# A graph kernel whose scalar engine forms part of the one-hot matrices

## The reference

```python
h = relu(layernorm(x)); x = x + L0(h)   # cosine similarity of both ends times edge weights, coeff[...] mix
h = relu(layernorm(x)); x = x + L1(h)   # three rounds of degree-normalised sums (LightGCN)
h = relu(layernorm(x)); x = x + L2(h)   # relu(x[src]) summed, two dense layers
h = relu(layernorm(x)); x = x + L3(h)   # sigmoid(edge_feature @ W_edge) gated mean
```

## Time and profile before

| | |
|---|---|
| median of 3 runs | 1308.59 us (1307.52 to 1309.86) |
| the profiled execution, its own time | 1321.73 us |
| its span, first to last instruction | 1319.8 us |
| mean granted clock of TensorE | 0.895 of full |
| busy: PE, DVE, ACT, POOL | 1060.3, 961.5, 632.8, 169.9 us |

### The profile page before, as it was taken

How to read it: one execution, slowest core, us unless ns; L and a number is a source line. 1 busy time by engine, 2 the same in 40 slices (tenths; PEclk the granted TensorE clock), 3 DMA queues, 4 the chain that set the end, 5 groups by cost and what they waited for, 6 DMA issues and landing times. The chain is left out here.

```text
span 1319.8 us, 36746 instructions
## 1 busy us (share of the span) xinstructions
PE 1060.3 (80%) x15699; PEld 797.3 (60%) x15699; DVE 961.5 (73%) x1434; ACT 632.8 (48%) x2058; POOL 169.9 (13%) x315
## 2 busy tenths in 40 slices
PE   1971558888887888888887888569999897999997
PEld 0620346666665666666665666369999885644553
DVE  8872389999999999999999998566669524233333
ACT  1830445555555555555555555189993212222222
POOL 4604411211112111211121111000000000000000
PEclk9795569988989998899998899679999897799999
DMA  9822301231123111221122111394000150266641
GB/s 227 220 38 32 98 28 77 101 128 77 77 81 147 78 77 77 119 110 77 77 108 120 77 77 77 120 396 188 2 2 2 74 227 2 80 227 242 249 150 25
DMA packets 37355, 144.82 MB, mean 110 GB/s; under 512 B 21148, under 2 KB 21692, under 8 KB 30268
## 3 DMA queue, kind: packets, MB, share of 16 engines
q1 hardware_dynamic: 32012, 133.20, 27.5%
q0 software_dynamic: 2912, 7.92, 2.2%
q10 hardware_dynamic: 2256, 1.23, 0.4%
HBM read 78.63 MB, written 63.71 MB: 108 GB/s over the span
## 5 line engine op out<-in xcount | busy, mean ns | idle before, releaser
L888 ACT ACTIVATE b_c_row<-b_ps 128x300 bf16<-128x300 f32 (+1 forms) x275 | 114.8, 417 | 244.9 <-PE b_ps L1073 229.3
L1286 PE MATMUL layers_ps<-layers_u,layers_c 128*128 128x192 bf16 x2500 | 213.6, 249 | 9.2 <-ACT layers_u L1465 6.7
L1073 PE MATMUL b_ps<-b_mv,b_soh 64*128 64x50 bf16 (+1 forms) x9600 | 202.8, 193 | 21.8 <-issue 12.0
L1073 PEld LDWEIGHTS b_ps<-b_mv,b_soh 64*128 64x128 bf16 x9600 | 172.7, 97 | 77.0 <-issue 43.3
L1286 PEld LDWEIGHTS layers_ps<-layers_u,layers_c 128*128 128x128 bf16 x2500 | 210.1, 99 | 15.0 <-DVE layers_y L1594 8.0
L1126 PE MATMUL b_ps<-k_ident,b_a_row 128*128 128x128 f32 x625 | 116.7, 309 | 89.6 <-DVE b_scale L999 88.5
L1073 PE MATMUL b_ps<-b_u_b,b_y 128*128 128x64 f32 x1250 | 164.8, 283 | 12.5 <-DVE b_y L1013 12.5
L1126 PEld LDWEIGHTS b_ps<-k_ident,b_a_row 128*128 128x128 f32 x625 | 73.6, 152 | 154.6 <-DVE b_scale L999 128.4
L1073 PEld LDWEIGHTS b_ps<-b_u_b,b_y 128*128 128x128 f32 x1250 | 151.1, 196 | 18.8 <-DVE b_y L1013 15.7
L976 DVE TENSOR_TENSOR b_mv<-b_mv,b_parts 128x2808 bf16<-128x2808 bf16 x100 | 149.3, 1493 | 0.0
L1741 DVE COPY layers_c<-layers_ps 128x512 f32<-128x512 f32 (+1 forms) x87 | 55.4, 637 | 117.8 <-PE layers_ps L1420 117.8
(11 more groups left out here) (253 smaller groups left out, 1146.9 us busy)
## 6 DMA issues: line engine op xcount, KB each, us to landing
g_blocks<-b_g_row SPq DMA_DIRECT2D x25, 1600.0 KB, 7.6
layers_c<-g_blocks SPq DMA_DIRECT2D x25, 1600.0 KB, 6.9
c_blocks<-b_c_row SPq DMA_DIRECT2D x25, 800.0 KB, 3.4
layers_c<-c_blocks SPq DMA_DIRECT2D x12, 1600.0 KB, 26.3
prep_attr<-in_edge_attr SPq DMA_DIRECT2D x2, 1883.0 KB
prep_attr<-in_edge_attr SPq DMA_DIRECT2D x1, 1876.0 KB
rec<-sort_rec SPq DMA_DIRECT2D x1, 1209.0 KB
layers_c<-c_blocks SPq DMA_DIRECT2D x1, 800.0 KB, 25.5
```

The source lines that it names most:

```text
L888: nc.scalar.activation(out, src[:, :, at, :, :], ACT.Copy).then_inc(s["evac"], 1)
L1073: return nc.tensor.matmul(out, lhsT, rhs, start=start, stop=True, skip_group_check=True)
L1286: return nc.tensor.matmul(out_, lhsT, rhs, start=start, stop=True, skip_group_check=True)
```

## The change

The low one-hots of the last quarter (10 columns) are no longer compared by DVE. POOL writes the negated low parts of those 10 columns to a small float tile `minus`. ACT then forms, for each of the columns, the square of (number minus low part), ten instructions of 128 elements, in place in `soh[1]`, and one instruction over all 1280 elements takes one minus that and rectifies it: 1 where the number is the low part, 0 elsewhere. In a step the squares are put behind the evacuation of lot 5 (five) and behind `positive` 2 (five), the last instruction behind the evacuation of lot 6. In block 0 all eleven stand behind the evacuation of lot 5. PE waits for the result ahead of lot 9. Elsewhere three semaphores are merged into others, with the same order of work.

```diff
+        minus = l.sb("minus", [P, OH[3][1] - OH[3][0]])
...
                 pool.wait_ge(s["onehot"], 4 * w + (o + 1))
+                if o == 3:
+                    if not (isinstance(w, int) and w == 0):
+                        pool.wait_ge(s["whole"], w)
+                    nc.gpsimd.tensor_tensor(minus[:, :], zero[:, 0:1].to_broadcast([P, n]),
+                                            cols(fld, b, lo, n)[:, 1, :], ALU.subtract).then_inc(s["lows"], 1)
...
+            def distances(w, c0, c1):
+                if c0 == 0:
+                    act.wait_ge(s["lows"], w + 1)
+                    act.wait_ge(s["lot"], NL * w + (ENDS[1] + NL))
+                for c in range(c0, c1):
+                    nc.scalar.activation(soh[1][:, c, :], k["numbers"][:, 0:P], ACT.Square, bias=minus[:, c:c + 1]).then_inc(s["near"], 1)
+
+            def equal(w):
+                n = OH[3][1] - OH[3][0]
+                act.wait_ge(s["near"], n * w + n)
+                nc.scalar.activation(soh[1][:, 0:n, :], soh[1][:, 0:n, :], ACT.Relu, bias=k["ones"][:, 0:1], scale=-1.0
+                                     ).then_inc(s["whole"], 1)
...
                     evacuate(r, w, 0, i)
+                    if i == 5:
+                        distances(w, 0, 10)
+                        equal(w)
...
                         evacuate(r, w, par, i)
+                        if i == 5:
+                            distances(w, 0, 5)
+                        if i == 6:
+                            equal(w)
                     if what == "sims":
                         positive(w - 1, i)
+                        if i == 2:
+                            distances(w, 5, 10)
...
-                nc.vector.tensor_tensor(halves(soh[b][:, 0:n, :]), nums(P), twice(1, P), ALU.is_equal)
+                if o < 3:
+                    nc.vector.tensor_tensor(halves(soh[b][:, 0:n, :]), nums(P), twice(1, P), ALU.is_equal)
...
                     pe.wait_ge(s["onehot"], 4 * w + (o + 3))
+                    if o == 3:
+                        pe.wait_ge(s["whole"], w + 1)
```

More of the change, by code:

```diff
@@ L192, in prepare @@
         names = ("iota const zero dst src weight attr param x dense cparam kept order find edge norm coefs gdiag whd rdiag "
-                 "compared signed tail stored firsts shift turned hd_act wht_pe whd_pe gate row_pe exp ln exps stds nrs "
-                 "sigmoid wht_act row_act scaled attr1 attr2")
+                 "compared signed tail stored shift turned hd_act wht_pe whd_pe gate exp ln exps stds nrs "
+                 "sigmoid wht_act scaled attr1 attr2")
         s = {n: l.sem(n) for n in names.split()}
@@ L323, in _ @@
             for i, (a, n) in enumerate(cuts):
-                act.wait_ge(s["row_pe"], i + 1)
-                nc.scalar.activation(rn_row[:, a:a + n], ps[:, 6 + i % 2, 0:n], ACT.Copy).then_inc(s["row_act"], 1)
+                act.wait_ge(s["wht_pe"], len(cuts) + i + 1)
+                nc.scalar.activation(rn_row[:, a:a + n], ps[:, 6 + i % 2, 0:n], ACT.Copy).then_inc(s["wht_act"], 1)
         @block.tensor
@@ L330, in _ @@
             pe.wait_ge(s["find"], 2)
-            nc.tensor.matmul(ps[:, 0, 0:P], k["ones"][:], diag[:], start=True, stop=True).then_inc(s["firsts"], 1)
+            nc.tensor.matmul(ps[:, 0, 0:P], k["ones"][:], diag[:], start=True, stop=True).then_inc(s["shift"], 1)
             pe.wait_ge(s["order"], 3)
@@ L369, in _ @@
                 if i >= 2:
-                    pe.wait_ge(s["row_act"], i - 1)
-                nc.tensor.matmul(ps[:, 6 + i % 2, 0:n], k["ones"][:], rdiag[:, i, 0:n], start=True, stop=True).then_inc(s["row_pe"], 1)
+                    pe.wait_ge(s["wht_act"], len(cuts) + i - 1)
+                nc.tensor.matmul(ps[:, 6 + i % 2, 0:n], k["ones"][:], rdiag[:, i, 0:n], start=True, stop=True).then_inc(s["wht_pe"], 1)
         @block.vector
@@ L405, in _ @@
             o(v.memset(z[:, T - 1:T], 0.0))
-            dve.wait_ge(s["firsts"], 1)
+            dve.wait_ge(s["shift"], 1)
             shape = [P, 2 * NJ, P]
@@ L411, in _ @@
             f(v.tensor_copy(at[:], line[:]))
-            dve.wait_ge(s["shift"], 1)
+            dve.wait_ge(s["shift"], 2)
             o(v.tensor_tensor(z[0:P - 1, T - 1:T], df[0:P - 1, T - 1:T], ps[0:P - 1, 1, 0:1], ALU.is_gt))
             o(v.tensor_reduce(total[:, 0:1], z[:], AX.X, ALU.add))
-            dve.wait_ge(s["shift"], 2)
+            dve.wait_ge(s["shift"], 3)
             o(v.tensor_scalar(total[:, 1:2], ps[:, 1, 0:1], 1.0, None, ALU.min))
@@ L523, in _ @@
             w(v.scalar_tensor_tensor(uD[:, :, :], whD[:, :, :], coef[:, 3:4], rn[:, :, None].to_broadcast(full), ALU.mult, ALU.mult))
-            dve.wait_ge(s["row_act"], len(cuts))
+            dve.wait_ge(s["wht_act"], 2 * len(cuts))
 def node_of(nc, c, rec, node):
@@ L687, in build @@
         names = ("index turned split rounded doubled hot onehot lot evac sims pos sgn weights made at scaled propped added "
-                 "gate deg degs peak rounds")
+                 "gate deg degs peak rounds lows near whole")
         s = {n: l.sem(n) for n in names.split()}
```

## The result

The changed kernel takes 1312.56 us (median of 20 runs), the kernel before, beside it, 1309.39 (20 runs). The ratio is 1.0023, with a 95% interval of 1.0013 to 1.0034: 3.0 us slower, between 1.7 and 4.5. The prediction said 1312.6 us and slower by over 0.2%.

What follows compares the result with a forecast made beforehand. In the steps it took PE's chain, not DVE (94% busy), to decide when `add` 1 starts. Steps 0, block 0 +4.0 and clock 0 on the median of 1308.59 gave 1312.6 us, range 1309.5 to 1317.

Steps and rivals of the forecast that it cites:

- DVE's instruction: Steps: removing DVE's comparison gains 0, at most 17.5 us; the wait ahead of `add` 1 grows from 0.75 to 1.48 us.
- The prices on ACT: ACT's new work: square pitch 0.28 us, bounds 0.20 and 0.38; rectifier 1.36 us, pitch 1.26; some 4.1 us a block.
- Room in the steps: Steps: ACT's new work costs 0, bounds 0 and 12 us; evacuation of lot 7 ends 0.9 us before lot 9.
- Block 0: Block 0: nothing hides ACT's eleven instructions between the evacuations of lots 5 and 6; +4.0 us, bounds 3.0 and 4.6.
- follows from there in one chain: End of block 0: after `turn_in` 2, at +4.3 us, DVE's split and the first step follow in one chain.
- The rival of a hidden delay: Block 0: faster ACT, transposes at high clock and a good clock pattern hide the delay; 1310.0 us, chance 0.20.
- The clock in the steps: Steps: a later start can change which steps the low clock stretches fall in; 0, bounds -0.8 to +1.0 us.
- DVE as the bound: Steps, at `add` 1: DVE is the bound, 0.73 us a step gained; 1295.1 us, chance 0.07 in whole or part.
- ACT awaited: Steps: ACT becomes the one awaited, 0.1 to 0.5 us a step, 2.4 to 12 us; 1315 to 1325, chance 0.13.
- The table load: Block 0: if the loaded table serves no square, one load of 1.28 us is added; 1313.9 us, chance 0.07.

Runs made afterwards that it cites:

- Two runs with more squares: Changed kernel with three, then eight more squares a step on ACT, into columns not read: 1320.58 us (ratio 1.0103) and 1361.09 us (1.0387).
- second profile: The kernel before, unchanged, profiled again: span 1307.0 us, with no PE wait for issue in block 0.
- `scale` 4 moved: DVE's `scale` 4 put ahead of `add` 1: kernel before 1298.77 us (0.9854), changed kernel 1304.34 us (0.9891); kernel before on another chip 1295.74 us (0.9893).
- steps-only: Changed kernel with block 0's comparison given back to DVE, the 24 steps keeping the new work: 1309.02 us, ratio 1.0010.
- block-0-only: Changed kernel with squares and rectifier taken out of the steps, DVE comparing there, block 0 keeping the new work: 1310.44 us, ratio 1.0025.
- comparison-less: Kernel before with DVE's comparison of the last quarter left out in the 24 steps, nothing in its place: 1308.90 us, ratio 1.0014.
- two entries moved: DVE's `scale` 4 and `sim` 2 both put ahead of `add` 1: kernel before 1323.78 us (1.0038), changed kernel 1325.28 us (1.0048).

## Why the prediction was right, point by point

**DVE's instruction: 0.** Right, and shown by itself. The stretch from `similar` 1 to `add` 1 kept its 5.66 us and the wait went from 0.75 to 1.48, the number that the prediction gave. Leaving the comparison out altogether gave 1.0014 (1.0000 to 1.0027). The busy share of 94% would have misled, the wait did not.

**The prices on ACT.** A square was priced at 0.38 us and is busy for 0.425; its pitch, which is what counts, was 0.28 and is 0.29. The rectifier was 1.36 and is 1.36 to 1.42. Together 4.1 predicted; in block 0, with the wait between them, 4.2 predicted and 4.32 measured. The formula of the Trainium skill, "ScalarE: Activation LUTs", section "What ACT_TABLE_LOAD costs", would have given a pitch of 0.29 and 1.35 for the rectifier, and the trace agrees; for the busy time of a square it gives 0.39, too low like the estimate. No table load came.

**Room in the steps.** Predicted 0.9 us ahead of lot 9; in the trace after, the evacuation of lot 7 ends at 512.94 + 0.48 = 513.42 and lot 9 starts at 514.24, 0.8. Lot 9 is 9.17 us behind `similar` 1, as it was before. Two runs with more squares bear out that the room ends there, though with three of them the price came through the clock, which the prediction's bound for this rival held without naming it.

**Block 0: +4.0.** The mechanism was right, shown by the two halves of the change and the traces; the term was mis-sized. `turn_in` 2 came 9.24 us behind the evacuation of lot 5, 4.2 more than the 5.01 of the first profile (evacuation of lot 5 at 154.30), but 3.7 more than the 5.55 of the second. The transposes gave back 1.1, where I took 0.3 off a delay of 4.3. So DVE's split was 2.6 us later against the second profile, 3.3 against the first. The lower bound of 3.0 was too high for executions without waits for issue ahead of this block. For those with them it was fair: on the second chip, where the profiles have them, it is 31.36 us from the evacuation of lot 5 to the first `similar` 0 in the kernel before with `scale` 4 moved, and 35.52 in the changed one with it, 4.2 more.

One link was wrong as well: that the first step "follows from there in one chain". The next `turn_in` also waits for its DMA, so of the delay at the split 1.3 us (against the steps-only kernel) to 2.6 us (against the second profile) reached the steps. The rival of a hidden delay didn't name this, and it came true in part.

**The clock in the steps: 0, bounds -0.8 to +1.0.** The bounds were too narrow for a single execution. The 23 steps from the first `similar` 0 to the 24th take 616.2 and 616.3 us in the two profiles of the kernel before, 618.2 in the one after, and 617.0, 619.7 and 619.1 in the steps-only, the block-0-only and the comparison-less kernel. `similar` 1 to `similar` 3 is 10.47 or 10.48 us in nearly all of them (10.56 and 10.73 once each in the changed kernel). It isn't that the clock was lower: its mean over these steps is 0.94 in the three longest and 0.93 in the three shortest. What differs is where its low stretches fall. Two stretches of the changed kernel, in the columns of the earlier trace rows:

```profile
200.50:207.30 6.80, 5.97 (x84) 3.75 (x85) 6.45 (x8) 2.17 (x4) 0.59 (x3) 0.50 0.36 144
255.10:282.40 27.30, 21.59 (x505) 16.84 (x499) 25.72 (x33) 19.46 (x51) 5.13 (x14) 1.00 0.28 116
```

The first begins 0.7 us ahead of a `similar` 0, and the time from there to the next `similar` 0 is 28.1 us; the second holds a whole step of 26.0. In the six profiles a low stretch of 3.4 us that begins up to 1.9 us behind `similar` 0 goes with 27.0 or 27.1 us, one of 6.8 us around it with 28.0 to 28.2, one of 6.8 us at the end of a step with 26.4 or 26.5, and one of 3.4 us that begins 5 us ahead of `similar` 0 with 26.0 (26.3 once), like none at all. A different start of the steps deals them out differently.

So some 1.9 us of the changed kernel's time can be this, beside 1.3 to 2.6 of block 0. How these 1.9 us stand in the median of many executions wasn't seen, as each kernel was profiled once, the kernel before twice. Even what lies behind the steps, which the change doesn't touch, took between 512.1 and 517.6 us in the same six profiles.

**The number.** That 1312.6 met 1312.56 to the tenth is luck. The kernel before came out 0.8 us slower than the three runs that I started from, and the difference 0.8 us smaller (3.2 between the medians in place of 4.0). Within the difference, block 0 was put 1.4 to 2.7 us too high and the steps perhaps 1.9 too low. What isn't luck is the sign and where the loss lies.

**The rivals.** DVE as the bound fell with the comparison-less kernel. ACT awaited fell for this change and came true with more squares. A delay in block 0 that is hidden altogether fell with the block-0-only kernel (1.0011 at the least); hidden in part, it stands. The table load didn't come.

## What to carry to other kernels

Before work is taken off an engine, look for the first wait behind it on that engine: here 0.75 us stood there in 24 of 24 steps, so 17.5 us of work could go and nothing moved. The same wait is where time can be won: ask which later work of that engine is ready by then, and put it in (16 us, by one entry). Work that is hidden in the steady loop must be looked up in the prologue too, since there nothing may hide it; and a prologue is worth a second profile, since here two executions of one kernel differed there by 12 us of waits.

## What the runs showed that was not expected

A shorter path made a slower kernel. With two entries moved the critical stretch got 0.84 us shorter, and the steps went from 25.0 and 26.3 us to a steady 27.3 when TensorE's granted clock fell to its low level (0.50 over 6.8 us) at the same place of each. Beside that, 23 steps of equal critical stretches summed to between 616.2 and 619.7 us by the places where the low stretches fell, the longer sums at the higher mean clock. A change of 0.2% in such a loop is no larger than this.
